# Attention stage of a hybrid block on one core: row scores, transposed scores and biases cut into 64x64 array tiles, the bias table split by head parity

## The chip, the core and the metric

The kernel runs on one core of one Trainium2 chip. The metric is the device time of one execution in microseconds (us), less is better. The core has TensorE (PE, with weight loads shown apart as PEld), VectorE (DVE), ScalarE (ACT), GpSimd (POOL) and the queue engine SyncE (SP), which issues most of the DMAs.

## What is computed

The block is attention, a mixture-of-experts layer, a Mamba layer and the same mixture-of-experts layer again. The change touches attention alone, for 2 sequences of 1024 tokens, 128 channels, 16 heads of 8 channels:

```python
def _L0_attn_a_ref(x, w_in, kernel_offsets, kernel_amplitudes, kernel_sharpness):
    ...
    q, k, v = (heads(q_), heads(k_), heads(v_))
    bias = tisa_bias(kernel_offsets, kernel_amplitudes, kernel_sharpness, l)
    scale = 1.0 / np.sqrt(HD).astype(np.float32)
    logits = jnp.einsum('bhld,bhmd->bhlm', q, k) * scale + bias[None]
    attn = jax.nn.softmax(logits, axis=-1)
    out = jnp.einsum('bhlm,bhmd->bhld', attn, v)
    return out.transpose(0, 2, 1, 3).reshape(b, l, d)
x = x + _L0_attn_a_ref(_layernorm(x, axis=-1), ...)
```

The bias of a head depends only on the distance of query and key (a Toeplitz matrix).

## The kernel before, in words

Every logit is computed twice. Once as **rows** (queries on the partitions, tile `at_rows`, three slots of a PSUM bank each), from which DVE takes each query's maximum with the bias table `table_max` (`pair_maxima`). Once as **columns** (keys on the partitions, tile `at_cols`, four banks): `scores` multiplies keys by queries, with the negated maximum in three further rows of the contraction (51 rows in all), and `biases` adds the bias by a matmul of `flip_sum` with the table `table_cols`. ACT takes the exponential into `prob`, and `products` multiplies `prob` by the values into `at_pv`.

Heads go in four groups of four; within a group two sequences; for each of them two halves of 512 queries and eight blocks of 128 keys. One (half, block) is a **step** (S = 0 to 127), and eight steps with one query half are a **phase** (16 phases). The q and k stacks hold the even heads of a group on partitions 0 to 47 and the odd ones on 64 to 111, so two matmuls (j = 0, 1) use the two halves of the array's rows.

The order on PE is written out by hand in `tensor_program`. A step is: one pair of row matmuls (`rows_pair`, n = 22 + 2S), the scores of both head pairs (hp = 0, 1), the biases of both, a second pair of rows, the products of the step before. In the third step of a phase the outputs of the phase before are turned (`turn_outputs`, L1308), in the seventh the negated maxima of the next one (`turn_maxima`, L1300). The last 11 steps have no rows left; there the order is scores, biases of hp 0, then scores, biases of hp 1. Waits: a row matmul waits until DVE has freed its slot (L1291); `scores(S, hp)` waits for the exponential of the step before and the same hp (L1316); ACT waits for the last bias matmul of hp (`cols_ready`).

`table_cols` holds for all four heads the high part of the bias on partitions 0 to 63 and the low part on 64 to 127; `flip_sum` (two reversed identities, one under the other) adds the two in one contraction over 128 rows. `load_table` (L1040) fills one of four chunks of columns by two DMAs from SP. Beside attention, weights of the next stage are split by POOL, and in the last two phases the first routing head of the next stage (`FfnHead`) runs among the steps.

Of the kernel before, what the change touches and what calls it, by code (L numbers as in the profile page):

```python
# [15 lines left out]
P = 128  # L16
# [879 lines left out]
def attention(m, x, w_in, offsets, amplitudes, sharpness, up_w, down_w, shared_up_w, shared_down_w,  # L896
# [3 lines left out]
    with ExitStack() as stage:  # L900
# [43 lines left out]
        t_col = sb("table_cols", [P, G4, COL_W], F16)  # L944
# [85 lines left out]
        def toeplitz(row, h0, nh, parts, c0, n):  # L1030

            a = row[h0:h0 + nh, c0:c0 + n]
            return bass.AP(tensor=a.tensor, offset=a.offset, ap=[[1, parts], [2 * L, nh], [1, n]])
# [6 lines left out]
        def load_table(eng, g, c):  # L1040
            for r, row in ((0, bias_hi), (HALF, bias_lo)):
                eng.dma_start(t_col[r:r + HALF, :, c * CW:(c + 1) * CW],
                              toeplitz(row, G4 * g, G4, HALF, c * CW, CW)).then_inc(tab_in[c], 16)
# [39 lines left out]
        with nc.Block() as block:  # L1083
# [147 lines left out]
            def tensor_program(pe):  # L1231
# [51 lines left out]
                def rows_pair(n):  # L1283

                    p, at = Pair(n), slots.start["pair", n]
                    if n % (2 * PHASE_PAIRS) == 0:
                        pe.wait_ge(stack_in[p.b], stack_count(p.g))
                    for j in range(2):
                        r = slice(HALF * j, HALF * j + QK_ROWS)
                        if at + j >= SLOTS:  # L1290
                            pe.wait_ge(slots_free, at + j + 1 - SLOTS)  # L1291
                        mm(s1[:, (at + j) % SLOTS, :], q_st[r, p.b, p.lh, p.hp, p.lbq * P:(p.lbq + 1) * P],  # L1292
                           k_st[r, p.b, p.hp, p.mh * BANK:(p.mh + 1) * BANK], start=True, stop=True).then_inc(fills, 1)
# [18 lines left out]
                def scores(S, hp):  # L1312
# [4 lines left out]
                    for j in range(2):  # L1317
                        r = slice(HALF * j, HALF * j + QK_ROWS + PIECES)
                        mm(s2[:, hp, j, :], k_st[r, b, hp, mb * P:(mb + 1) * P],  # L1319
                           q_st[r, b, lh, hp, :], start=True, stop=False)  # L1320

                def biases(S, hp):
                    for j in range(2):
                        for u in range(2):
                            c = step_columns(S % STEPS, u)
                            last = mm(s2[u * HALF:(u + 1) * HALF, hp, j, :], m.flip_sum[:],  # L1326
                                      t_col[:, 2 * hp + j, c:c + BANK], start=False, stop=True)
                    last.then_inc(cols_ready, 1)
# [29 lines left out]
                for S in range(ALL_STEPS):  # L1358
# [8 lines left out]
                    if pairs:  # L1367
                        for hp in range(2):
                            scores(S, hp)
                        if phase_turned_in(S) is not None:  # L1370
                            turn_maxima(phase_turned_in(S))
                        if it % BATCH == 0:
                            for c in range(CHUNKS):
                                if chunk_starts[c] == s:
                                    pe.wait_ge(tab_in[c], 32 * (it // BATCH + 1))
                        for hp in range(2):
                            biases(S, hp)
                        for n in pairs[1:]:
                            rows_pair(n)
                    else:  # L1380
                        for hp in range(2):
                            scores(S, hp)
                            biases(S, hp)
                            if hp == 0 and phase_turned_in(S) is not None:
                                turn_maxima(phase_turned_in(S))
# [700 lines left out]
```

## Time and profile before

| | |
|---|---|
| time, three runs | 1118.01, 1123.06, 1123.2 us (median 1123.06) |
| span of the profiled execution | 1119.0 us (the profile gives no other time of it) |
| TensorE busy in the span | 975.8 us, 87% |
| VectorE busy | 853.2 us, 76% |
| ScalarE busy | 677.5 us, 61% |
| GpSimd busy | 487.5 us, 44% |
| mean granted TensorE clock | 0.931 of full |

A busy share is an average over four stages. Attention lies between 0 and about 517 us; its 128 steps between 70 and 505 us. In a timeline a row is a run of the same instruction: start, length, engine, line, what is written and read, how often, and in brackets how long the engine idled before it and what ended that. Starts of matmuls are recorded, their ends are modelled, so distances between starts are what counts.

### The profile page before, as it was taken

Reading aid. Unit: us, or ns where it says so; the run is one execution under the profiler, and the core shown is the slowest. Engines: PE = TensorE matmul, PEld = TensorE weight load, DVE = VectorE, ACT = ScalarE, POOL = GpSimd, SP = SyncE. Lnnn points to the kernel's source line nnn. Section 1 sums busy time; section 2 is a strip of 40 time slices with the busy share of each in tenths; the row PEclk is TensorE's granted clock in tenths of the full one; section 3 lists DMA queues with packets and bytes.
Section 4 is the critical chain, followed back from the end, with each engine's and each line's share of the span. In section 5 each row is a group of like instructions: output and inputs, shape, how many; then the busy total and the mean of one; then the engine's idle time right before and its main releaser. Section 6 shows DMA issues by size and latency. Waiting matters only on the chain. (4 is left out here: it accounts for less than half of the span.)

```text
span 1119.0 us, 17095 instructions
## 1 busy us (share of the span) xinstructions
PE 975.8 (87%) x5565; PEld 543.6 (49%) x5565; DVE 853.2 (76%) x2203; ACT 677.5 (61%) x1042; POOL 487.5 (44%) x454
## 2 busy tenths in 40 slices
PE   4889999999999999994999999972777449999998
PEld 2413232223222322323777888731566337778886
DVE  7688888889888988766798555477897787975543
ACT  4226656565656565562668888768334126788886
POOL 4400101101110110101788999814674027889997
PEclk9559999999999999996999999987899659999999
DMA  4930224131313230003466677300000035676973
GB/s 100 281 107 9 79 71 85 35 101 55 71 34 104 53 70 2 1 2 87 143 177 175 160 198 191 96 20 1 0 0 0 3 93 151 172 179 158 218 197 96
DMA packets 80086, 105.65 MB, mean 94 GB/s; under 512 B 17741, under 2 KB 41091, under 8 KB 80003
## 3 DMA queue, kind: packets, MB, share of 16 engines
q1 hardware_dynamic: 78119, 102.42, 35.7%
q10 hardware_dynamic: 1883, 2.21, 0.7%
q8 instruction: 42, 0.69, 0.3%
q14 instruction: 42, 0.34, 0.1%
HBM read 95.84 MB, written 8.52 MB: 93 GB/s over the span
## 5 line engine op out<-in xcount | busy, mean ns | idle before, releaser
L663 POOL TENSOR_TENSOR f_act_low<-f_act,f_act_high 128x512 fp32r<-128x512 f32 x272 | 353.0, 1315 | 151.2 <-ACT f_act_high L639 143.5
L1506 DVE CUSTOM_DVE_ANT_0 at_rows<-at_rows,at_table_max 128x512 f32<-128x512 f32 x512 | 340.0, 718 | 43.6 <-PE at_rows L1292 42.9
L1452 ACT ACTIVATE at_prob<-at_cols 128x1024 f32<-128x1024 f32 x256 | 248.2, 1021 | 185.8 <-PE at_cols L1326 185.8
L678 DVE SCALAR_TENSOR_TENSOR f_gated<-f_hid,f_cw 128x512 f32<-128x512 f32 x256 | 174.0, 687 | 115.1 <-ACT f_act L644 86.9
L644 ACT ACTIVATE f_act<-f_gated 128x512 f32<-128x512 f32 x272 | 171.7, 631 | 110.2 <-DVE f_gated L678 78.5
L639 ACT CAST f_act_high<-f_act 128x512 fp32r<-128x512 f32 x272 | 164.7, 606 | 0.0
L1326 PE MATMUL at_cols<-at_table_cols,flip_sum 128*64 128x512 f16 x1024 | 139.3, 389 | 0.0
L1338 PE MATMUL at_pv<-at_prob,at_v_stack 128*32 128x512 f32 x1024 | 137.2, 608 | 0.2 <-ACT at_prob L1452 0.2
L1292 PE MATMUL at_rows<-at_k_stack,at_q_stack 48*128 48x512 bf16 x512 | 122.5, 408 | 12.8 <-DVE at_maxima L1506 10.1
L610 PE MATMUL f_acc<-f_act_high,wd_high 128*128 128x512 f32 x272 | 109.4, 402 | 9.0 <-POOL f_act_low L663 8.8
L1292 PEld LDWEIGHTS at_rows<-at_k_stack,at_q_stack 48*128 48x128 bf16 x512 | 28.9, 93 | 170.2 <-DVE at_maxima L1506 116.8
L610 PE MATMUL f_acc<-f_act_low,wd_high 128*128 128x512 f32 x272 | 106.8, 393 | 0.0
L610 PE MATMUL f_acc<-f_act_high,wd_low 128*128 128x512 f32 x272 | 106.7, 392 | 0.0
L600 PE MATMUL f_hid<-f_x_high,wu_high 128*128 128x512 f32 x204 | 81.9, 401 | 0.0
L1319 PE MATMUL at_cols<-at_q_stack,at_k_stack 51*128 51x512 bf16 x512 | 80.7, 382 | 0.7 <-ACT at_prob L1452 0.7
L1220 POOL CAST wu_high<-at_raw_weights 128x512 fp32r<-128x512 f32 (+1 forms) x9 | 5.3, 591 | 173.6 <-DMA at_raw_weights<-in_L_ffn_down_w_dram 154.0
L600 PE MATMUL f_hid<-f_x_high,wu_low 128*128 128x512 f32 x204 | 80.7, 395 | 0.0
L600 PE MATMUL f_hid<-f_x_low,wu_high 128*128 128x512 f32 x204 | 80.6, 395 | 0.0
L1326 PEld LDWEIGHTS at_cols<-at_table_cols,flip_sum 128*64 128x64 f16 x1024 | 48.1, 109 | 64.6 <-issue 42.1
L1506 DVE DVE_READ_ACCUMULATOR2_ANT at_maxima<- 128x1 f32 x512 | 71.8, 140 | 0.0
L1200 POOL COPY at_v_stack<-at_v_nat 128x256 f32<-128x256 f32 x8 | 3.1, 398 | 152.6 <-PE at_pv L1338 144.6
L610 PEld LDWEIGHTS f_acc<-f_act_high,wd_high 128*128 128x128 f32 x272 | 51.4, 189 | 28.5 <-POOL f_act_low L663 18.3
(322 smaller groups left out, 1351.0 us busy)
## 6 DMA issues: line engine op xcount, KB each, us to landing
f_cw<-f_c_rows SPq DMA_DIRECT2D x256, 256.0 KB, 4.5
at_table_cols<-bias_rows SPq DMA_DIRECT2D x32, 248.0 KB, 5.1
at_table_max<-bias_rows SPq DMA_DIRECT2D x12, 480.0 KB, 4.6
at_q_stack<-q_parts SPq DMA_DIRECT2D x32, 96.0 KB, 2.5
at_k_stack<-k_parts SPq DMA_DIRECT2D x24, 96.0 KB, 3.8
at_raw_weights<-in_L_ffn_up_w_dram SPq DMA_DIRECT2D x8, 256.0 KB, 4.3
at_raw_weights<-in_L_ffn_down_w_dram SPq DMA_DIRECT2D x8, 256.0 KB, 4.9
at_table_max<-bias_rows ACTq DMA_DIRECT2D x4, 480.0 KB, 8.0
```

Source lines behind the costliest of these rows:

```text
L600: last = nc.tensor.matmul(hid[:, n % HID_SLOTS, :], w[:, unit.pp, :], x[:, cols], start=(k == 0), stop=(k == 2))
L610: last = nc.tensor.matmul(acc[:, unit.j, :], w[:, unit.pp, :], x[:, s, :], start=(unit.pp == 0 and k == 0), stop=(unit.pp == NPAIRS - 1 an ...
L639: nc.scalar.copy(act_h[:, n % PART_SLOTS, :], act[:, n % ACT_SLOTS, :]).then_inc(u.high_done, 1)
L644: nc.scalar.activation(act[:, n % ACT_SLOTS, :], gated[:, n % GATE_SLOTS, :], ACT.Square).then_inc(u.square_done, 1)
L663: nc.gpsimd.tensor_tensor(act_l[:, n % PART_SLOTS, :], act[:, n % ACT_SLOTS, :], act_h[:, n % PART_SLOTS, :].bitcast(F32), ALU.subtract).t ...
L678: ins = nc.vector.scalar_tensor_tensor(out=gated[:, n % GATE_SLOTS, :], in0=hid[:, n % HID_SLOTS, :], scalar=0.0, in1=cw[:, k % C_SLOTS, u ...
L1292: mm(s1[:, (at + j) % SLOTS, :], q_st[r, p.b, p.lh, p.hp, p.lbq * P:(p.lbq + 1) * P], k_st[r, p.b, p.hp, p.mh * BANK:(p.mh + 1) * BANK], s ...
L1319: mm(s2[:, hp, j, :], k_st[r, b, hp, mb * P:(mb + 1) * P], q_st[r, b, lh, hp, :], start=True, stop=False)
L1326: last = mm(s2[u * HALF:(u + 1) * HALF, hp, j, :], m.flip_sum[:], t_col[:, 2 * hp + j, c:c + BANK], start=False, stop=True)
L1338: last = mm(pv[32 * h:32 * h + 32, :], vst[:, it % 2, LT - 1 - s % LT, h, :], prob[:, S % 2, h, :], start=(s % LT == 0), stop=(s % LT == L ...
L1452: act(prob[:, S % 2, 2 * hp:2 * hp + 2, :], s2[:, hp, :, :], ACT.Exp).then_inc(exp_done, 1)
L1506: nc.vector.tensor_tensor_reduce(out=slot, in0=slot, in1=t_max[:, 2 * p.hp + j, c:c + BANK][:, ::-1], scale=1.0, scalar=-3.0e38, op0=ALU.a ...
```

## The change

Three matmuls become 64x64 tiles. `rows_pair` and `scores` split their 128 output partitions into two matmuls of 64 (c, u), so a set of four matmuls covers the four quarters of the array. `table_cols` becomes [half by head parity][piece][head pair][column]: even heads on partitions 0 to 63, odd ones on 64 to 127, high and low part behind one another. `biases` takes 64 rows for each matmul and adds the high and the low part one after the other, 16 matmuls instead of 8. `load_table` issues four DMAs of half the size for each chunk. The order of the last 11 steps becomes that of the others (scores of both hp, then biases of both).

```diff
-        t_col = sb("table_cols", [P, G4, COL_W], F16)
+        t_col = sb("table_cols", [P, 2, G4 // 2, COL_W], F16)
...
         def load_table(eng, g, c):
-            for r, row in ((0, bias_hi), (HALF, bias_lo)):
-                eng.dma_start(t_col[r:r + HALF, :, c * CW:(c + 1) * CW],
-                              toeplitz(row, G4 * g, G4, HALF, c * CW, CW)).then_inc(tab_in[c], 16)
+            for j in range(2):
+                for piece, row in enumerate((bias_hi, bias_lo)):
+                    eng.dma_start(t_col[HALF * j:HALF * (j + 1), piece, :, c * CW:(c + 1) * CW],
+                                  toeplitz(row, G4 * g + j, G4 // 2, HALF, c * CW, CW)).then_inc(tab_in[c], 16)
...
-                        mm(s1[:, (at + j) % SLOTS, :], q_st[r, p.b, p.lh, p.hp, p.lbq * P:(p.lbq + 1) * P],
-                           k_st[r, p.b, p.hp, p.mh * BANK:(p.mh + 1) * BANK], start=True, stop=True).then_inc(fills, 1)
+                        for c in range(2):
+                            q0 = p.lbq * P + c * HALF
+                            last = mm(s1[c * HALF:(c + 1) * HALF, (at + j) % SLOTS, :],
+                                      q_st[r, p.b, p.lh, p.hp, q0:q0 + HALF],
+                                      k_st[r, p.b, p.hp, p.mh * BANK:(p.mh + 1) * BANK], start=True, stop=True)
+                        last.then_inc(fills, 1)
...
-                        mm(s2[:, hp, j, :], k_st[r, b, hp, mb * P:(mb + 1) * P],
-                           q_st[r, b, lh, hp, :], start=True, stop=False)
+                        for u in range(2):
+                            k0 = mb * P + u * HALF
+                            mm(s2[u * HALF:(u + 1) * HALF, hp, j, :], k_st[r, b, hp, k0:k0 + HALF],
+                               q_st[r, b, lh, hp, :], start=True, stop=False)
 
                 def biases(S, hp):
-                    for j in range(2):
-                        for u in range(2):
-                            c = step_columns(S % STEPS, u)
-                            last = mm(s2[u * HALF:(u + 1) * HALF, hp, j, :], m.flip_sum[:],
-                                      t_col[:, 2 * hp + j, c:c + BANK], start=False, stop=True)
+
+                    for piece in range(2):
+                        for j in range(2):
+                            half = slice(HALF * j, HALF * (j + 1))
+                            for u in range(2):
+                                c = step_columns(S % STEPS, u)
+                                last = mm(s2[u * HALF:(u + 1) * HALF, hp, j, :], m.flip_sum[half, :],
+                                          t_col[half, piece, hp, c:c + BANK], start=False, stop=piece == 1)
                     last.then_inc(cols_ready, 1)
...
-                    else:
-                        for hp in range(2):
-                            scores(S, hp)
-                            biases(S, hp)
-                            if hp == 0 and phase_turned_in(S) is not None:
-                                turn_maxima(phase_turned_in(S))
+                    for hp in range(2):
+                        biases(S, hp)
+                    for n in pairs[1:]:
+                        rows_pair(n)
```

On PE, one step in the middle of the kernel before reads as follows: rows, scores, biases, rows, products (the shape is output partitions x columns).

```order
L1292 MATMUL at_rows<-at_k_stack,at_q_stack 128x512 x2
L1319 MATMUL at_cols<-at_q_stack,at_k_stack 128x512 x4
L1326 MATMUL at_cols<-at_table_cols,flip_sum 64x512 x8
L1292 MATMUL at_rows<-at_k_stack,at_q_stack 128x512 x2
L1338 MATMUL at_pv<-at_prob,at_v_stack 32x512 x4
```

The same step of the changed kernel, in which the lines of the file have moved on:

```order
L1295 MATMUL at_rows<-at_k_stack,at_q_stack 64x512 x4
L1326 MATMUL at_cols<-at_q_stack,at_k_stack 64x512 x8
L1336 MATMUL at_cols<-at_table_cols,flip_sum 64x512 x16
L1295 MATMUL at_rows<-at_k_stack,at_q_stack 64x512 x4
L1348 MATMUL at_pv<-at_prob,at_v_stack 32x512 x4
```

The order of the five groups is the same; rows, scores and biases now have the same output width, and twice the matmuls.

On PE, one of the last 11 steps of the kernel before:

```order
L1319 MATMUL at_cols<-at_q_stack,at_k_stack 128x512 x2
L1326 MATMUL at_cols<-at_table_cols,flip_sum 64x512 x4
L1319 MATMUL at_cols<-at_q_stack,at_k_stack 128x512 x2
L1326 MATMUL at_cols<-at_table_cols,flip_sum 64x512 x4
L1338 MATMUL at_pv<-at_prob,at_v_stack 32x512 x4
```

And of the changed one:

```order
L1326 MATMUL at_cols<-at_q_stack,at_k_stack 64x512 x8
L1336 MATMUL at_cols<-at_table_cols,flip_sum 64x512 x16
L1348 MATMUL at_pv<-at_prob,at_v_stack 32x512 x4
```

Here the biases of hp 0 have moved behind the scores of hp 1.

On SP's queue, the first load of the table (the difference, - before, + changed), ahead of the stores of the second sequence's parts and the send of the first maxima:

```order
-L1115 DMA at_k_stack<-at_two_ones 3x16x128 x2
-L1042 DMA at_table_cols<-bias_rows 64x4x496 x8
+L1116 DMA at_k_stack<-at_two_ones 3x16x128 x2
+L1043 DMA at_table_cols<-bias_rows 64x2x496 x16
 L1025 DMA k_parts<-at_parts 128x3x1024
```

The number of table DMAs doubles and each has half the heads; nothing else in this queue changes place.

## Rows read from the trace of the kernel before

**Rows 1.** Page, part 1: busy us, share of the span, instructions.

```profile
PE 975.8 (87%) x5565; PEld 543.6 (49%) x5565; DVE 853.2 (76%) x2203; ACT 677.5 (61%) x1042; POOL 487.5 (44%) x454
```

**Rows 2.** Windows: length, busy us (instructions) of each engine, clock, DMA share, GB/s.

```profile
70.00:505.00 435.00, 423.66 (x3196) 128.00 (x3195) 372.46 (x1184) 260.49 (x277) 38.03 (x46) 0.99 0.20 50
...
180.34:206.74 26.40, 26.04 (x203) 7.93 (x201) 23.57 (x75) 15.99 (x17) 0.40 (x1) 1.00 0.28 60
...
148.46:151.52 3.06, 3.06 (x26) 0.83 (x25) 2.78 (x8) 1.81 (x3) 0.00 (x0) 1.00 0.02 4
...
866.06:871.06 5.00, 5.00 (x48) 5.00 (x47) 3.92 (x16) 2.23 (x4) 0.00 (x0) 1.00 0.01 3
```

**Rows 3.** Timeline of PE, one step, from scores to the next scores.

```profile
149.68 0.60 PE L1319 MATMUL at_cols<-at_q_stack,at_k_stack 51*128 51x512 bf16 x4
150.21 1.05 PE L1326 MATMUL at_cols<-at_table_cols,flip_sum 128*64 128x512 f16 x8
151.20 0.39 PE L1292 MATMUL at_rows<-at_k_stack,at_q_stack 48*128 48x512 bf16 x2
151.52 1.06 PE L1338 MATMUL at_pv<-at_prob,at_v_stack 128*32 128x512 f32 x8
152.51 0.39 PE L1292 MATMUL at_rows<-at_k_stack,at_q_stack 48*128 48x512 bf16 x2
152.74 0.60 PE L1319 MATMUL at_cols<-at_q_stack,at_k_stack 51*128 51x512 bf16 x4
```

**Rows 4.** Timeline, 150.44 to 150.46 us: a weight load while bias matmuls run.

```profile
150.45 0.11 PEld L1326 LDWEIGHTS at_cols<-at_table_cols,flip_sum 128*64 128x64 f16 x2
```

**Rows 5.** Timeline of ACT, and of PEld, in the next step.

```profile
151.79 1.02 ACT L1452 ACTIVATE at_prob<-at_cols 128x1024 f32<-128x1024 f32 x1
153.93 1.94 ACT L1452 ACTIVATE at_prob<-at_cols 128x1024 f32<-128x1024 f32 x2 [1.12 <-PE at_cols L1326]
...
152.86 0.10 PEld L1319 LDWEIGHTS at_cols<-at_q_stack,at_k_stack 51*128 51x128 bf16 x2 [0.24 <-ACT at_prob L1452]
```

**Rows 6.** Timeline of DVE, then PE, in the step after an output turn.

```profile
188.89 0.14 DVE L1506 DVE_READ_ACCUMULATOR2_ANT at_maxima<- 128x1 f32 x1
...
189.11 0.39 PE L1292 MATMUL at_rows<-at_k_stack,at_q_stack 48*128 48x512 bf16 x2
```

**Rows 7.** Timeline of DVE, then PE, behind the chain that negates the maxima.

```profile
196.91 0.69 DVE L1506 CUSTOM_DVE_ANT_0 at_rows<-at_rows,at_table_max 128x512 f32<-128x512 f32 x1
...
196.96 0.39 PE L1292 MATMUL at_rows<-at_k_stack,at_q_stack 48*128 48x512 bf16 x1
197.71 0.39 PE L1292 MATMUL at_rows<-at_k_stack,at_q_stack 48*128 48x512 bf16 x1 [0.36 <-DVE at_maxima L1506]
```

**Rows 8.** Timeline of PE: the turn of the maxima.

```profile
199.78 0.24 PE L1300 MATMUL at_rows<-identb,at_negm 128*48 128x128 bf16 x1
199.79 1.09 PE L1326 MATMUL at_cols<-at_table_cols,flip_sum 128*64 128x512 f16 x8
```

**Rows 9.** Timeline of PE in the last steps: products of two neighbouring steps.

```profile
489.94 1.07 PE L1338 MATMUL at_pv<-at_prob,at_v_stack 128*32 128x512 f32 x8
...
492.68 1.07 PE L1338 MATMUL at_pv<-at_prob,at_v_stack 128*32 128x512 f32 x8
```

**Rows 10.** Timeline of DVE: the first work behind the last products.

```profile
505.04 0.26 DVE L1542 RECIPROCAL at_rden<-at_rows 128x16 f32<-128x16 f32 x1 [8.80 <-PE at_rows L1308]
```

**Rows 11.** Timeline of SP's queue around the first table load.

```profile
41.59 5.41 SPq L1042 DMA_DIRECT2D at_table_cols<-bias_rows  x8
...
51.16 2.18 SPq L1025 DMA_DIRECT2D q_parts<-at_parts  x1
64.49 0.79 SPq L1058 DMA_DIRECT2D at_q_stack<-at_negT  x1
```

**Rows 12.** Timeline, 326 to 336 us: the longest stall of a step.

```profile
328.82 1.13 DVE L1524 CAST at_negm<-at_mtop 128x16 bf16<-128x16 f32 x1
...
331.43 0.53 PE L1292 MATMUL at_rows<-at_k_stack,at_q_stack 48*128 48x512 bf16 x1 [2.00 <-DVE at_maxima L1506]
```

More of the change, by code:

```diff
@@ L1030, in toeplitz @@
         def toeplitz(row, h0, nh, parts, c0, n):
-            a = row[h0:h0 + nh, c0:c0 + n]
-            return bass.AP(tensor=a.tensor, offset=a.offset, ap=[[1, parts], [2 * L, nh], [1, n]])
+            a = row[h0:h0 + 1, c0:c0 + n]
+            return bass.AP(tensor=a.tensor, offset=a.offset, ap=[[1, parts], [2 * 2 * L, nh], [1, n]])
         def load_max_tables(eng, g, hp):
@@ L1366, in tensor_program @@
                         pe.wait_ge(max_in[s // LT], 32 * (it + 1))
-                    if pairs:
-                        for hp in range(2):
-                            scores(S, hp)
-                        if phase_turned_in(S) is not None:
-                            turn_maxima(phase_turned_in(S))
[L1372 to L1376, printed above, removed]
-                            biases(S, hp)
-                        for n in pairs[1:]:
-                            rows_pair(n)
-                    else:
-                        for hp in range(2):
-                            scores(S, hp)
-                            biases(S, hp)
-                            if hp == 0 and phase_turned_in(S) is not None:
-                                turn_maxima(phase_turned_in(S))
+                    for hp in range(2):
+                        scores(S, hp)
+                    if phase_turned_in(S) is not None:
+                        turn_maxima(phase_turned_in(S))
+                    if it % BATCH == 0:
+                        for c in range(CHUNKS):
+                            if chunk_starts[c] == s:
+                                pe.wait_ge(tab_in[c], 64 * (it // BATCH + 1))
+                    for hp in range(2):
+                        biases(S, hp)
+                    for n in pairs[1:]:
+                        rows_pair(n)
                     if S > 0:
```

## The prediction

> **What bounds the kernel now.** First the busy shares: PE 87%, DVE 76%, ACT 61% of the whole span [rows 1]. That is a mean over four stages, so next the windows. In attention's 128 steps, 435 us, PE is busy for 423.7, DVE for 372.5, ACT for 260.5 [rows 2]. Within one undisturbed phase PE is busy 26.04 of 26.40 us and DVE 23.57, a reserve of 2.8 us for DVE; in one step PE is busy for all 3.06 us [rows 2]. The reader should see PE as the bound, but with DVE close behind.
>
> Next the timeline of one step [rows 3], read by distances between starts: scores to biases 0.53 us, biases to rows 0.99, rows to products 0.32, products to rows 0.99, rows to scores 0.23; sum 3.06. Between the last two groups the shape of the tiles does not change, and a set of matmuls that fill the array together costs 0.22 to 0.23; 512 columns at the upper clock of 2.4 GHz, which the granted clock of 1.00 in this step [rows 2] is, are 0.213. Scores are two such sets (0.43 to 0.44), biases four (0.85 to 0.88). So wherever the tile shape changes, 0.09 to 0.14 us are lost: scores to biases 0.09 to 0.10, biases to rows 0.11 to 0.14, rows to products 0.10, and a like amount inside the 0.99 of the products. That is what the change can remove.
>
> Last, who else is near. ACT: the weights of the second score group are loaded at 152.86, when the exponential that began at 151.79 and took 1.02 has ended (152.81); the biases start at 153.27, the next exponential at 153.93, and two of them take 1.94, to 155.87 [rows 3, 5]. From end to end that is 3.06 again: ACT's loop has hardly any more reserve than PE, though ACT is only 61% busy. (The start at 153.27 is one step of 3.06 behind the 150.21 of [rows 3].)
>
> **The change part by part.**
>
> *Work of the sets.* Rows stay one set for a pair (four quarter matmuls in place of two halves), scores two sets, biases four (16 quarters in place of 8 halves). If four quarters run together as two halves did, this costs nothing. PE has no such form in this trace; the nearest are the products, four tiles of 128x32 together, and the rows, two of 64x128. I take 0.
>
> *Changes of shape.* Of four in a step the two between scores, biases and rows go. With 0.22 for a set they are worth 0.09 + 0.11 = 0.20 us, with 0.213 they are 0.10 + 0.14 = 0.24 [rows 3]. I take 0.21, since a little comes back where 64-column weights must be loaded behind the products. PE's step is then 2.85.
>
> *Weight loads.* They double, four for each set. A load of 64 columns takes 0.11 us. The row at 150.45 stands in the middle of the bias matmuls, which run from 150.21 to 151.26: the load of a later matmul is hidden behind the one in flight, on the same rows of the array [rows 3, 4]. Taken as 0; if not hidden, the price is up to 0.11 a set.
> The Trainium skill (TensorE: Matmul & The Clock Gate, Part 3, What overlaps and what doesn't) states that weight loads overlap with matmuls in flight only if they go to another row group. By that rule each of the 8 sets would show its load, 0.9 us in a step. The trace speaks against it: the load at 150.45 overlaps on all 128 rows. I follow the trace.
>
> *ACT's loop.* The change takes the shape change out of it too: 152.86, one set 0.22, biases start, 0.64 to the exponential (0.66 now, less a little), 1.94, and 0.05 to the next load: 2.85. So ACT allows just the same step as PE.
>
> *DVE.* Two places in a phase don't follow PE. (a) Behind the output turn DVE works without a gap; the slot for the row matmul at 189.11 is free at 188.89 + 0.14 + some 0.05 = 189.08 [rows 6]. With a step shorter by 0.21 it would be wanted at 188.90: 0.18 of this step's 0.21 is given back. (b) Behind the chain that negates the maxima the second row matmul runs at 197.71, 0.80 after DVE took up its work at 196.91, instead of right behind the first at 196.96 [rows 7]. The start of DVE's chain hangs on an earlier row pair, so PE comes earlier and waits longer: this step's 0.21 is given back whole.
>
> *Turn of the maxima.* L1300 stands between scores and biases. Now it starts 0.01 ahead of the biases [rows 8], for both are narrow tiles over 128 rows; after the change it is a shape of its own between two equal ones, and a further change of 0.10 plus its own 128 columns, 0.05, comes in. This step keeps some 0.07.
>
> Phase of eight steps: five at 0.21, one at 0.03, one at 0, one at 0.07: 1.15 us. Thirteen undisturbed phases give 15.0. Of phase 0 six steps count, 1.2; of phase 14 the first three, 0.4, before the routing head's DVE work sets the pace. Sum 16.6.
>
> *The last 11 steps.* They take 2.74 now [rows 9], with six shape changes. PE would need less: 6 sets at 0.22, products 0.99 and 0.10 make 2.41. But the order is now both scores ahead of both biases, so the first exponential of a step hangs on the second one of the step before, and ACT's loop of 2.85 holds here too: 11 x 0.11 = 1.2 us lost. These steps do set the end: DVE sits idle for 8.80 us before it gets the last outputs [rows 10].
>
> *SP.* The first table load becomes 16 DMAs. Eight take 5.41 us to issue; 16 take between 5.4 (cost by size) and 10.8 (cost by piece), so up to 5.4 more. Behind them queue the stores of the second sequence, the last issued at 51.16 and done at 53.3, and the send of the first maxima at 64.49, which waits for DVE: 11 us of cover [rows 11]. Without that cover PE would start its steps late by the whole 5.4. Later loads come while a chunk is not wanted for four steps or more. 0.
>
> Sum: -16.6 + 1.2 = -15.4, say -15. The span was 1119.0 and the runs 1118.0 to 1123.2, median 1123.06, 4 us above the span, so the same difference from the median gives **1108 us**.
>
> **The rivals.**
>
> *DVE and ACT keep half.* If the two waits behind DVE grow and spread to their neighbours, or ACT's loop is 2.95 instead of 2.85 because the load at 152.86 must be finished before its matmul (0.10), the step is 2.95 and the gain 0.11: -8 + 2 (last steps), 1117 us. For it: two engines end within 0.05 us of each other in [rows 5]. Against: row matmuls at 197.71 start with their load, without 0.10 between. Chance 0.12.
>
> *No difference.* Quarter tiles cost a little each: 0.02 to 0.03 for each of 8 sets cancels 0.21. For it: with 64-column tiles the four sets of biases take 0.99, and I cannot say from groups how much of the 0.14 is the change of shape and how much the sets. 1117 to 1126, about 1122. Chance 0.16.
>
> *Slower, by weight loads.* The loads of four quarters don't hide: 8 x 0.11 = 0.87 in each of 117 steps, less the 0.21, and 6 x 0.11 in the last: +77 and +6, about 1205 us. It decides from 0.03 us a set. Against it [rows 4]. This is what the rule cited above would give. Chance 0.07.
>
> *Slower, by the feed of instructions.* A step would hold 32 quarter matmuls and 8 records of products, each with a load: 80 records in 2.85 us, 36 ns each. Now there are 51 in 3.06 (60 ns), and the densest 5 us of the whole trace have 95 (53 ns) [rows 2]; nothing in the trace shows 36 over a longer time. At 53 ns the step is 4.2 us: +1.2 x 117, about 1260 us. It decides above 38 ns. Against: weight loads of one set are recorded together, so PE itself takes them fast. Chance 0.08.
>
> *Slower by something small*, such as a lower granted clock for a while or the stall of [rows 12] at more places: there a cast of DVE took 1.13 us and PE waited 2.00. Where POOL's weight splits meet DVE's short chain depends on when each is due, and all moves. 3 us more or less in any case; 1130 to 1140 where it happens several times. Chance 0.05.
>
> **How the numbers follow.** The forecast has 0.49, half kept 0.12, no difference 0.16, the slower cases 0.20, and 0.03 is left for more than forecast: without (a) and (b), 117 x 0.21 = 24.6, 1100 us. A measurement of this kernel tells about 0.5%, 5.6 us, from no change. Faster holds the forecast, the larger gain and most of the half: 0.63. Same 0.17, slower 0.20. The forecast's own range is 1102 to 1114. The range for 8 in 10 begins at 1099 and reaches through "no difference" to 1127; the slower cases beyond (0.18) are left out.
>
> **What would show it.** Right: distances of starts in a plain step of 0.43 to 0.45 from scores to biases, 0.86 to 0.88 from biases to rows, unchanged 0.32 and 0.99; a step of 2.85, a phase of 25.2 to 25.3, DVE still busy for 23.6 of it; a row matmul waiting some 0.95 behind the negated maxima; 2.85 in the last steps, ACT idle between its pairs for 0.9. Wrong: biases to rows above 0.95 (sets or loads cost more), gaps in PE that nothing released (feed), a step at 3.06 with PE idle before the second scores (ACT) or before rows at all steps (DVE), the first step beginning later than now (SP).

## The result and the profile after

The changed kernel takes **1105.99 us** (median of four runs, 1103.68 to 1109.1) against 1121.36 us for the kernel before on the same chip (four runs, 1118.01 to 1123.2): a ratio of 0.989, 95% interval 0.986 to 0.9919. A second set of runs gave 1104.45 against 1118.28, 0.9871 [0.9837, 0.9905]. Forecast were 1108 us and 1099 to 1127.

The page, part 1, of the changed kernel (busy us, share of the span, instructions), whose profiled execution has a span of 1107.4 us and a time of 1109.1:

```profile
PE 957.4 (86%) x7613; PEld 561.8 (51%) x7613; DVE 855.9 (77%) x2203; ACT 677.8 (61%) x1042; POOL 487.8 (44%) x454
```

TensorE has 2048 matmuls more and is busy for 18 us less [rows 1]. Windows of one undisturbed phase and of one plain step (the columns of [rows 2]):

```profile
172.30:197.82 25.52, 24.98 (x333) 8.97 (x329) 23.65 (x75) 16.00 (x18) 2.07 (x3) 1.00 0.27 58
173.34:176.23 2.89, 2.89 (x45) 0.99 (x40) 2.75 (x9) 1.94 (x3) 0.79 (x2) 1.00 0.59 85
```

The phase fell from 26.41 (the 26.40 of [rows 2]) to 25.52, the step from 3.06 to 2.89; VectorE is busy for 23.65 us, nearly as before (23.57). Timeline of PE, the step that answers to [rows 3]:

```profile
173.34 0.64 PE L1326 MATMUL at_cols<-at_q_stack,at_k_stack 51*64 51x512 bf16 x8
173.81 1.04 PE L1336 MATMUL at_cols<-at_table_cols,flip_sum 64*64 64x512 f16 x16
174.67 0.39 PE L1295 MATMUL at_rows<-at_k_stack,at_q_stack 48*64 48x512 bf16 x4
174.99 1.07 PE L1348 MATMUL at_pv<-at_prob,at_v_stack 128*32 128x512 f32 x8
175.99 0.41 PE L1295 MATMUL at_rows<-at_k_stack,at_q_stack 48*64 48x512 bf16 x4
176.23 0.39 PE L1326 MATMUL at_cols<-at_q_stack,at_k_stack 51*64 51x512 bf16 x4
```

From scores to biases it is now 0.47 us (before 0.53), from biases to rows 0.86 (0.99), the other three 0.32, 1.00 and 0.24 (0.32, 0.99, 0.23). The 16 bias matmuls run as four sets of four and take 0.86, 0.215 a set; 512 columns at 2.4 GHz are 0.213. The ACT part of the same step, and the load of its second scores, which answer to [rows 5]:

```profile
172.50 1.02 ACT L1455 ACTIVATE at_prob<-at_cols 128x1024 f32<-128x1024 f32 x1
174.46 1.94 ACT L1455 ACTIVATE at_prob<-at_cols 128x1024 f32<-128x1024 f32 x2 [0.95 <-PE at_cols L1336]
...
173.57 0.11 PEld L1326 LDWEIGHTS at_cols<-at_q_stack,at_k_stack 51*64 51x64 bf16 x4 [0.32 <-ACT at_prob L1455]
```

The exponential ends at 173.52, the load of the second scores starts at 173.57, the biases 0.24 later at 173.81, the next exponential 0.65 after that, and two of them take 1.94. From end to end that is 2.89, the step. In steps in which the second scores don't wait, such as those whose scores start at 170.49 and 180.13 us, scores to biases is 0.43 instead of 0.47. So **ACT's loop sets the plain step now**, by a small margin over PE.

The last step's first exponential starts at 500.15 us before and at 485.81 after. Where these 14.3 us come from, by the distances of each step's first exponential:

| part | before | after | forecast of the difference |
|---|---|---|---|
| start of the steps | 73.00 | 70.60 | 0 |
| phase 0 | 27.61 | 26.44 | -1.2 |
| phases 1 to 13 | 347.85 | 336.51 | -15.0 |
| phase 14 | 31.47 | 31.52 | -0.4, and part of the +1.2 |
| phase 15 | 20.23 | 20.75 | part of the +1.2 |
| from there to the end | 618.8 | 621.6 | 0 |

The start and the end differ from run to run whatever the kernel: over all profiles here the start lies at 68.0 to 73.1, the rest at 617.0 to 621.8. What the edit did to the steps is the middle four rows: -11.9 us.

Two further profiles of the same work on PE, x8 below for the kernel before and the second one of the changed kernel, give -13.6 us for these rows.

An undisturbed phase, step by step:

| step | 1 | 2 | 3 | 4 | 5 | 6 | 7 | 8 | sum |
|---|---|---|---|---|---|---|---|---|---|
| before | 3.06 | 4.07 | 3.06 | 3.06 | 3.06 | 3.86 | 3.19 | 3.06 | 26.41 |
| after | 2.89 | 3.86 | 3.07 | 2.89 | 2.89 | 4.08 | 2.95 | 2.89 | 25.52 |

Step 2 (here by the order of its exponentials) holds the output turn, step 6 the chain that negates the maxima, step 7 their turn. PE in steps 6 and 7, which answers to [rows 7, 8]:

```profile
190.26 0.38 PE L1295 MATMUL at_rows<-at_k_stack,at_q_stack 48*64 48x512 bf16 x2
191.19 0.40 PE L1295 MATMUL at_rows<-at_k_stack,at_q_stack 48*64 48x512 bf16 x2 [0.54 <-DVE at_maxima L1509]
...
192.75 0.60 PE L1326 MATMUL at_cols<-at_q_stack,at_k_stack 51*64 51x512 bf16 x8
193.29 0.24 PE L1305 MATMUL at_rows<-identb,at_negm 128*48 128x128 bf16 x1
193.45 1.06 PE L1336 MATMUL at_cols<-at_table_cols,flip_sum 64*64 64x512 f16 x16
194.34 0.49 PE L1295 MATMUL at_rows<-at_k_stack,at_q_stack 48*64 48x512 bf16 x4
```

The second row matmul of the pair comes 0.93 behind the first (0.75 before), for PE arrives earlier and DVE does not. And DVE, the six operations of the chain:

```profile
189.06 0.14 DVE L1509 DVE_READ_ACCUMULATOR2_ANT at_maxima<- 128x1 f32 x1
189.24 0.18 DVE L1524 TENSOR_REDUCE at_mtop<-at_maxima 128x16 f32<-128x32 f32 x1
189.46 0.17 DVE L1525 TENSOR_SCALAR at_negm<-at_mtop 128x16 bf16<-128x16 f32 x1
189.67 0.17 DVE L1526 SCALAR_TENSOR_TENSOR at_mtop<-at_mtop,at_negm 128x16 f32<-128x16 f32 x1
189.88 0.17 DVE L1527 CAST at_negm<-at_mtop 128x16 bf16<-128x16 f32 x1
190.09 0.18 DVE L1528 TENSOR_TENSOR at_mtop<-at_mtop,at_negm 128x16 f32<-128x16 f32 x1
190.30 0.17 DVE L1529 CAST at_negm<-at_mtop 128x16 bf16<-128x16 f32 x1
190.38 0.69 DVE L1509 CUSTOM_DVE_ANT_0 at_rows<-at_rows,at_table_max 128x512 f32<-128x512 f32 x1
```

Each waits for the one before and so costs 0.21, though it works for 0.17. No row read starts between the accumulator read at 189.06 and 190.38; the slot that PE waits for is freed only behind it.

### The profile page after: what moved, and what is told of

It reads as the page before. It is cut to its first block and busy times, and to the rows that moved or that the text cites. A ratio compares the mean times of both kernels' runs of the same rounds, so it can differ in the third digit from the quotient of the medians.

```text
span 1107.4 us, 21223 instructions
## 1 busy us (share of the span) xinstructions
PE 957.4 (86%) x7613; PEld 561.8 (51%) x7613; DVE 855.9 (77%) x2203; ACT 677.8 (61%) x1042; POOL 487.8 (44%) x454
## 5 line engine op out<-in xcount | busy, mean ns | idle before, releaser
L1295 PE MATMUL at_rows<-at_k_stack,at_q_stack 48*64 48x512 bf16 x1024 | 128.3, 413 | 16.9 <-DVE at_maxima L1509 15.2
L1336 PE MATMUL at_cols<-at_table_cols,flip_sum 64*64 64x512 f16 x2048 | 135.4, 380 | 0.0
L1295 PEld LDWEIGHTS at_rows<-at_k_stack,at_q_stack 48*64 48x64 bf16 x1024 | 36.4, 107 | 146.1 <-DVE at_maxima L1509 124.7
L1326 PE MATMUL at_cols<-at_q_stack,at_k_stack 51*64 51x512 bf16 x1024 | 82.9, 387 | 2.9 <-ACT at_prob L1455 2.9
L1336 PEld LDWEIGHTS at_cols<-at_table_cols,flip_sum 64*64 64x64 f16 x2048 | 59.0, 107 | 42.3 <-issue 1.9
```

The costliest lines, as they stand in the source:

```text
L1295: last = mm(s1[c * HALF:(c + 1) * HALF, (at + j) % SLOTS, :], q_st[r, p.b, p.lh, p.hp, q0:q0 + HALF], k_st[r, p.b, p.hp, p.mh * BANK:(p.mh ...
L1326: mm(s2[u * HALF:(u + 1) * HALF, hp, j, :], k_st[r, b, hp, k0:k0 + HALF], q_st[r, b, lh, hp, :], start=True, stop=False)
```

## The experiments

The questions were four. Is the gain the removed changes of shape, and what is one worth (x1 to x4)? Does ACT's loop hold the step and the tail (x1, x5)? What holds steps 6 and 7 (x7, x9, x10)? What are the disturbed phases (x6)? In all of them "step" is the distance of first exponentials, from the trace. They ran in three sets, in which the kernel before had medians of 1116.82 us (x1 to x4), 1118.28 (x6 to x8 and the second runs of the changed kernel) and 1116.75 (x5, x9, x10); across sets the ratios are to be compared, not the times.

**x1: both orders on the changed kernel.**

```diff
-                    for hp in range(2):
-                        scores(S, hp)
-                    if phase_turned_in(S) is not None:
-                        turn_maxima(phase_turned_in(S))
...
                     for hp in range(2):
+                        scores(S, hp)
                         biases(S, hp)
+                        if hp == 0 and phase_turned_in(S) is not None:
+                            turn_maxima(phase_turned_in(S))
```

> The changed kernel with its 64x64 tiles, but in every step scores and biases of head pair 0, then scores and biases of head pair 1 (nothing is left out). Theory (ACT's loop holds the plain step at 2.89 us and the last steps too): the second scores now stand 0.43 us later, PE no longer waits for the exponential, a plain step falls to 2.85, a last step from 2.89 to about 2.41; about -4 and -5 us against the changed kernel's 1106, so 1096 to 1099. Rival (quarter tiles or the feed of instructions hold the step at 2.89): the steps stay at 2.89 and 1106 is measured.

1103.75 us (1100.55 to 1107.54), ratio 0.9875 [0.9846, 0.9903]. The plain step is 2.86, the last steps 2.42 instead of 2.89, but step 7 rose from 2.95 to 3.24, so the phase is 25.44. Expected were 1096 to 1099 us, and that did not come: phases 1 to 13 are only 0.4 us shorter than in the changed kernel (336.16 against 336.51), and the 3.8 us that phases 14 and 15 lose by the trace (48.52 against 52.27) do not stand out in the times. PE of one plain step of x1:

```profile
155.06 0.39 PE L1326 MATMUL at_cols<-at_q_stack,at_k_stack 51*64 51x512 bf16 x4
155.28 0.60 PE L1336 MATMUL at_cols<-at_table_cols,flip_sum 64*64 64x512 f16 x8
155.71 0.39 PE L1326 MATMUL at_cols<-at_q_stack,at_k_stack 51*64 51x512 bf16 x4
155.93 0.60 PE L1336 MATMUL at_cols<-at_table_cols,flip_sum 64*64 64x512 f16 x8
156.37 0.39 PE L1295 MATMUL at_rows<-at_k_stack,at_q_stack 48*64 48x512 bf16 x4
```

Between equal shapes a change of operand costs nothing: 0.22, 0.43, 0.22, 0.44. 2.86 is PE's own step, so ACT's loop costs the changed kernel 0.03 in a plain step and 0.47 in a last one.

**x2: the same order on the kernel before**, where it adds two changes of shape to each step.

```diff
-                        for hp in range(2):
-                            scores(S, hp)
-                        if phase_turned_in(S) is not None:
-                            turn_maxima(phase_turned_in(S))
...
                         for hp in range(2):
+                            scores(S, hp)
                             biases(S, hp)
+                            if hp == 0 and phase_turned_in(S) is not None:
+                                turn_maxima(phase_turned_in(S))
```

> The kernel before with only the order within a step changed: scores, biases of head pair 0, then scores, biases of head pair 1 (nothing left out). Two more changes of tile shape in each of 117 steps. Theory (each change costs about 0.1 us): step 3.26 instead of 3.06, 20 to 25 us slower than before, about 1143. Rival (the 0.09 to 0.14 belong to the bias matmuls themselves, such as their first weight load, and not to the change of shape): four sets of biases cost the same wherever they stand, under 5 us of difference.

1137.87 us (1135.17 to 1141.06), ratio 1.017 [1.0134, 1.0207]. The step went from 3.06 to 3.28, +0.22 for two more changes. PE of one step of x2:

```profile
152.77 0.38 PE L1319 MATMUL at_cols<-at_q_stack,at_k_stack 51*128 51x512 bf16 x2
153.08 0.62 PE L1326 MATMUL at_cols<-at_table_cols,flip_sum 128*64 128x512 f16 x4
153.64 0.39 PE L1319 MATMUL at_cols<-at_q_stack,at_k_stack 51*128 51x512 bf16 x2
153.96 0.62 PE L1326 MATMUL at_cols<-at_table_cols,flip_sum 128*64 128x512 f16 x4
154.51 0.39 PE L1292 MATMUL at_rows<-at_k_stack,at_q_stack 48*128 48x512 bf16 x2
```

Distances 0.31, 0.56, 0.32, 0.55, where x1 has 0.22, 0.43, 0.22, 0.44: each crossing costs 0.09 to 0.13, in both directions. In the 117 steps that have rows this order adds 21 us to the kernel before; x1 has it in these steps too (and in the last 11, where the kernel before had it all along) and stays about where the changed kernel was (0.9875, beside 0.989 and 0.9871): the change of shape is the price, not the order.

**x3 and x4: half of the change.** x3 is the changed kernel with the rows left 128 wide; its edit is shown. x4 has the rows and the scores left so, and only the biases and their table in 64x64.

```diff
-                        for c in range(2):
-                            q0 = p.lbq * P + c * HALF
-                            last = mm(s1[c * HALF:(c + 1) * HALF, (at + j) % SLOTS, :],
-                                      q_st[r, p.b, p.lh, p.hp, q0:q0 + HALF],
-                                      k_st[r, p.b, p.hp, p.mh * BANK:(p.mh + 1) * BANK], start=True, stop=True)
-                        last.then_inc(fills, 1)
+                        mm(s1[:, (at + j) % SLOTS, :], q_st[r, p.b, p.lh, p.hp, p.lbq * P:(p.lbq + 1) * P],
+                           k_st[r, p.b, p.hp, p.mh * BANK:(p.mh + 1) * BANK], start=True, stop=True).then_inc(fills, 1)
```

> The changed kernel with the row matmuls put back to two of 64x128, scores and biases left as 64x64. Theory (any difference of shape costs, width too): rows to scores and biases to rows get 0.1 us each back, step 3.05 to 3.08, about 1119 to 1122, all the gain gone. Rival (only the change between 128 and 64 rows of the array costs, the width is free): step stays at 2.89, 1106.

> The kernel before with the bias table split by head parity and 16 bias matmuls of 64x64, rows and scores left as 64x128, order of the last steps as changed. Theory (any difference of shape costs): as many changes as before, step 3.05, and the last steps a little slower: 1120 to 1124. Rival (only the number of rows matters): all three kinds have 64 rows, step 2.89, 1106.

x3: 1121.48 us, ratio 1.0033 [1.001, 1.0055], step 3.06. x4: 1122.5 us, ratio 1.0042 [1.0018, 1.0067], step 3.06. PE of one step of x3:

```profile
152.21 0.39 PE L1293 MATMUL at_rows<-at_k_stack,at_q_stack 48*128 48x512 bf16 x2
152.53 0.63 PE L1322 MATMUL at_cols<-at_q_stack,at_k_stack 51*64 51x512 bf16 x8
152.98 1.03 PE L1332 MATMUL at_cols<-at_table_cols,flip_sum 64*64 64x512 f16 x16
153.95 0.39 PE L1293 MATMUL at_rows<-at_k_stack,at_q_stack 48*128 48x512 bf16 x2
```

Rows to scores is 0.32 here, 0.24 in the changed kernel; biases to rows 0.97, there 0.86. Width alone, on equal array rows, is a change of shape. Parts of the edit give nothing: either way four crossings are left in a step. Only with all three alike do two go. Both halves are even a little slower than the kernel before. Part of it is the new order of the last steps, which they keep: phases 14 and 15 take 52.54 us in x3 and 53.56 in x4, 51.70 before.

**x8: the DMAs alone**, the kernel before with each table DMA cut in two.

```diff
-                eng.dma_start(t_col[r:r + HALF, :, c * CW:(c + 1) * CW],
-                              toeplitz(row, G4 * g, G4, HALF, c * CW, CW)).then_inc(tab_in[c], 16)
+                for h in (0, 2):
+                    eng.dma_start(t_col[r:r + HALF, h:h + 2, c * CW:(c + 1) * CW],
+                                  toeplitz(row, G4 * g + h, 2, HALF, c * CW, CW)).then_inc(tab_in[c], 16)
...
-                                    pe.wait_ge(tab_in[c], 32 * (it // BATCH + 1))
+                                    pe.wait_ge(tab_in[c], 64 * (it // BATCH + 1))
```

> The kernel before with each DMA of the bias table for the columns cut into two by head pairs, nothing else (nothing left out). Theory (hidden behind SP's idle time): 16 DMAs take 5 us more to issue at the start, the first exponential does not come later for it, no difference, within 3 us. Rival (SP's queue is on the path at the start or at a chunk change): 3 to 6 us slower, first exponential later or steps 5 or 13 of some group longer.

1119.63 us, ratio 1.0007 [0.9986, 1.0027]: no difference that can be told.

**x6: POOL's splits three steps later**, on x1.

```diff
-WEIGHT_STEPS = tuple(4 + 12 * k for k in range(1 + PAIRS // WPAIRS))
+WEIGHT_STEPS = tuple(7 + 12 * k for k in range(1 + PAIRS // WPAIRS))
```

> The changed kernel in the order of x1 (scores and biases head pair by head pair), and the steps in which SP loads the next stage's weights moved from 4 + 12k to 7 + 12k (nothing left out). Theory (the irregular steps, in x1 3.63, 4.30, 5.07, 4.18 and 4.76 us in phases 2, 8, 9, 11 and 12, come where POOL's weight split meets DVE's short dependent operations behind a phase's last maxima or its outputs): the splits fall elsewhere, these five go back to 3.07 and 3.83, phases 1 to 13 together 336.2 falls by about 4, time some 4 us under x1. Rival (they come of DMA traffic or of DVE itself): the same steps stay long.

1098.49 us (1096.29 to 1102.6), ratio 0.982 [0.9791, 0.9849], beside 0.9875 for x1; in the profiles phases 1 to 13 fell by 3.5 us (336.16 to 332.62), where 4 were expected. What the splits collide with shows in the changed kernel in phase 12, whose sixth step takes 5.14; DVE, PE and POOL there:

```profile
395.56 1.24 DVE L1525 TENSOR_SCALAR at_negm<-at_mtop 128x16 bf16<-128x16 f32 x1
...
398.35 0.40 PE L1295 MATMUL at_rows<-at_k_stack,at_q_stack 48*64 48x512 bf16 x2 [1.61 <-DVE at_maxima L1509]
...
395.50 1.27 POOL L1223 TENSOR_TENSOR wd_low<-at_raw_weights,wd_high 128x512 fp32r<-128x512 f32 x1
```

A DVE operation of 0.17 us took 1.24, from shortly after POOL's started to just after it ended, and PE's wait rose from 0.54 to 1.61. What phases 1 to 13 take above 13 times their median (0.9 us of it in phase 13, where the next stage's statistics start) is 4.5 us in the kernel before, 4.2 and 2.8 in two profiles of the changed one, 2.1 to 9.1 over the ten profiles with the splits in their old place, and 1.5, 1.8 and 1.6 in the three with the later splits (x6, x9, x10). It differs between runs of one kernel, so which step is hit, and how hard, is luck; that less is lost with the later splits holds in all three.

Not all of this is the wait itself. In the kernel before, PE waited 2.00 us in the stall of [rows 12], and behind it the granted clock was 0.51 from 331.50 to 335.00 us, that is 1.2 GHz nearly throughout. The products that start there take 1.93 us instead of 1.07:

```profile
331.89 1.93 PE L1338 MATMUL at_pv<-at_prob,at_v_stack 128*32 128x512 f32 x8
```

Of the 3.1 us by which this phase is too long, about half is the wait and half the lower clock. The same happened once in x8 and twice in x3, behind waits of 1.92 to 2.07 us, which is how x3 comes to 9.1. Behind the 1.61 us above, and behind 1.82 in x1, the clock stayed at 1.00; why it falls in one case and not in the other is not shown.

**x7: a short chain**, on the changed kernel. The expectation says what it leaves out.

```diff
-                    ch.link(ts(piece(0), top(0), -1.0, None, ALU.mult))
-                    ch.link(stt(out=top(1), in0=top(0), scalar=-1.0, in1=piece(0), op0=ALU.mult, op1=ALU.subtract))
-                    ch.link(nc.vector.tensor_copy(piece(1), top(1)))
-                    ch.link(tt(top(2), top(1), piece(1), ALU.subtract))
-                    nc.vector.tensor_copy(piece(2), top(2)).then_inc(negm_ready, 1)
+                    ch.add(ts(piece(0), top(0), -1.0, None, ALU.mult))
+                    ch.add(ts(piece(1), top(0), 0.0, None, ALU.mult))
+                    ts(piece(2), top(0), 0.0, None, ALU.mult).then_inc(negm_ready, 1)
```

> The changed kernel with the chain that negates the maxima cut from six dependent operations to four of which three do not wait for each other; the second and third part of the maxima are left as zero. Theory (the second row matmul behind the chain waits for DVE, so this step follows the chain's length): the chain is 0.4 to 0.5 us shorter, step 6 of a phase falls from 4.08 by just that to about 3.6, a phase to 25.1, 6 us in all. Rival (PE or ACT hold that step): 4.08 stays.

1093.93 us (1089.4 to 1095.92), ratio 0.9767 [0.9729, 0.9805]. From the first negation to the next row read it is 0.24 us now (184.50 to 184.74) instead of 0.92, and step 6 fell from 4.08 to 3.39, while all other steps stayed: the chain's length is this step's, one to one. The saving was underestimated: expected were 0.4 to 0.5 a phase and 6 us, measured 0.69 and, against the changed kernel in the same set (1104.45), 10.5. Nine of them are the step in 13 phases; phase 0 fell by more than its one step (from 26.88 to 23.74), because the clock rose earlier in it, as told at the end.

**x9: the same saving without leaving anything out**, on x6: the second part is written as bf16 straight from the sum.

```diff
-                    ch.link(stt(out=top(1), in0=top(0), scalar=-1.0, in1=piece(0), op0=ALU.mult, op1=ALU.subtract))
-                    ch.link(nc.vector.tensor_copy(piece(1), top(1)))
-                    ch.link(tt(top(2), top(1), piece(1), ALU.subtract))
-                    nc.vector.tensor_copy(piece(2), top(2)).then_inc(negm_ready, 1)
+                    ch.add(stt(out=top(1), in0=top(0), scalar=-1.0, in1=piece(0), op0=ALU.mult, op1=ALU.subtract))
+                    ch.link(stt(out=piece(1), in0=top(0), scalar=-1.0, in1=piece(0), op0=ALU.mult, op1=ALU.subtract))
+                    tt(piece(2), top(1), piece(1), ALU.subtract).then_inc(negm_ready, 1)
```

> On top of x6: in the chain that negates the maxima the first bf16 part and the rest below it are taken straight from the sum instead of one from the other, so 5 operations instead of 6 with one dependent step less. Theory (in each phase one step waits for the end of this chain, so its length is this step's): the sixth step of a phase falls from 3.83 to about 3.5, the phase from 25.4 to 25.1, 13 phases make 4 to 4.5 us: about 1094. Rival (DVE's next row reads are what the row pair waits for, not the chain itself): the step stays at 3.8 and the time at 1098.

**1092.01 us** (1086.53 to 1096.08), ratio 0.9773 [0.9747, 0.9799], the lowest median of a kernel that computes everything. Step 6 is 3.50, the phase 25.11. DVE in x9:

```profile
185.91 0.17 DVE L1524 TENSOR_SCALAR at_negm<-at_mtop 128x16 bf16<-128x16 f32 x1
186.12 0.18 DVE L1525 SCALAR_TENSOR_TENSOR at_mtop<-at_mtop,at_negm 128x16 f32<-128x16 f32 x1
186.21 0.17 DVE L1526 SCALAR_TENSOR_TENSOR at_negm<-at_mtop,at_negm 128x16 bf16<-128x16 f32 x1
186.41 0.17 DVE L1527 TENSOR_TENSOR at_negm<-at_mtop,at_negm 128x16 bf16<-128x16 f32 x1
186.51 0.69 DVE L1508 CUSTOM_DVE_ANT_0 at_rows<-at_rows,at_table_max 128x512 f32<-128x512 f32 x1
```

From the first negation to the first row read it is 0.60 here and 0.92 in the changed kernel (189.46 to 190.38): two operations that don't wait for each other start 0.09 apart, not 0.21. The 0.32 is the fall of step 6 (3.83 to 3.50). Between the profiles of x6 and x9, phases 1 to 13 are 4.4 us shorter, as expected, and phase 0 another 2.2, where the granted clock reached 1.00 some 4 us earlier (below). The medians are 6.5 us apart, the ratios of the two sets 5.

**x10: the turn beside the products**, on x9. The order of the slots and DVE's copy move with it (not shown).

```diff
+                    if phase_turned_in(S) is not None:
+                        turn_maxima(phase_turned_in(S))
                     for n in pairs[:1]:
                         rows_pair(n)
...
-                        if hp == 0 and phase_turned_in(S) is not None:
-                            turn_maxima(phase_turned_in(S))
```

> On top of x9: the turn of the maxima (128 columns, output of 48 partitions) moves from between scores and biases to the start of its step, directly behind the products, where the shape of the tiles changes in any case; the copy on DVE moves with it. Theory (each shape change costs 0.10 to 0.11 us wherever it stands): the seventh step falls from 3.24 to about 3.0 and 13 phases give 3 us: about 1091. Rival (the turn then waits for DVE's negated maxima, or the row pair behind it waits longer for its slot, since the turn takes a slot of the rows' bank): what is won is given back, 1094 or more.

1093.87 us (1088.52 to 1097.36), ratio 0.9787 [0.976, 0.9813]; x9 on the same chip 0.9773. Step 7 fell from 3.24 to 2.87, more than expected, but step 6 rose from 3.50 to 4.11, and the phase is 25.35 instead of 25.11: the rival, by the trace. The times alone can't tell the two apart, since their intervals overlap. PE and PEld in x10:

```profile
189.94 0.24 PE L1305 MATMUL at_rows<-identb,at_negm 128*48 128x128 bf16 x1
190.10 0.85 PE L1295 MATMUL at_rows<-at_k_stack,at_q_stack 48*64 48x512 bf16 x4
...
190.55 0.11 PEld L1295 LDWEIGHTS at_rows<-at_k_stack,at_q_stack 48*64 48x64 bf16 x2 [0.34 <-DVE at_maxima L1508]
```

The turn takes a slot of the rows' bank in a place where DVE is behind, so the second matmul of the pair behind it waits at 190.55 for a row read, and with it all of the step.

**x5: the tail alone**, the changed kernel with the old order in the last 11 steps.

```diff
-                    for hp in range(2):
-                        scores(S, hp)
...
-                    for hp in range(2):
-                        biases(S, hp)
+                    if pairs:
+                        for hp in range(2):
+                            scores(S, hp)
...
+                        for hp in range(2):
+                            biases(S, hp)
+                    else:
+                        for hp in range(2):
+                            scores(S, hp)
+                            biases(S, hp)
+                            if hp == 0 and phase_turned_in(S) is not None:
+                                turn_maxima(phase_turned_in(S))
```

> The changed kernel with only the order of the last 11 steps put back (scores and biases of hp 0, then of hp 1). Theory (ACT's loop of 2.89 sets these steps in the changed kernel, since both scores stand ahead of both biases): the last steps fall from 2.89 to the 2.42 that PE needs, 9 or 10 plain ones of them, 4 to 5 us less than the changed kernel, about 1100. Rival (in these steps the products, or the routing head's work on DVE, are what holds): the steps stay at 2.85 or more and the time at 1104 to 1106.

1101.9 us (1098.5 to 1104.1), ratio 0.9855 [0.9831, 0.988]. The last steps take 2.42, and phases 14 and 15 together 48.34 us instead of 52.27: 3.9 less, as the theory had it. This rests on the trace: the ratio is only 0.0016 below that of the changed kernel in another set (0.9871), less than the intervals are wide.

## Why the prediction was right

The 1108 us were 2 us from the median, and the mechanism was the one forecast. Its steps one by one:

*Sets and weight loads at 0.* Right. Four bias sets take 0.86 with four quarters each, and their 16 loads of 64 columns are hidden behind matmuls in flight:

```profile
173.65 0.71 PEld L1336 LDWEIGHTS at_cols<-at_table_cols,flip_sum 64*64 64x64 f16 x16
```

The weight-load rival fell, and with it the rule of the Trainium skill that was cited beside it (TensorE: Matmul & The Clock Gate, Part 3, What overlaps and what doesn't): here loads overlap matmuls on the same rows of the array.

*Two crossings worth 0.21.* Right: PE's own step is 2.86 (x1), 0.20 below 3.06; two more cost 0.22 (x2); four left give 3.06 (x3, x4). So in "no difference" the 0.02 to 0.03 a set is refuted too: the sets of 64 columns are not what the 0.99 held.

*ACT's loop 2.85.* The mechanism was right, the size off by 0.04: it is 2.89, the biases 0.24 behind the load and the exponential 0.65 behind them, where 0.22 and 0.64 were taken. In four of the eight steps this is what remains: 0.17 instead of 0.21. The half-kept rival's 2.95 did not come, since the second scores start with their load.

*DVE.* (a) Step 3 went from 3.06 to 3.07: all of its 0.21 was given back, 0.18 were forecast. (b) was half seen. The forecast was 0 for step 6 and -0.07 for step 7; measured +0.22 and -0.24. Only their sum is DVE's: 7.05 before, 7.03 after, 7.07 in x1, and between 7.03 and 7.16 in all ten profiles with the chain of six, where 6.98 was forecast. From 190.38 to 194.44 DVE has no gap, and the row pair at 194.34 takes 0.42 to the products instead of 0.32, since its second matmul needs the turn's slot, which DVE's copy frees then. So what the turn kept was given back there. Where the chain got shorter, the sum fell: 6.34 in x7, 6.74 in x9.

*Phase gain 1.15.* Mis-sized: 0.89. Four steps give 0.17, step 2 gives 0.21, steps 3, 6 and 7 nothing. This is the term of the sum that was off: -15.0 for 13 phases, of which the step sizes make -11.6 and the traces show -11.3.

*Phase 0 -1.2, phase 14 -0.4, last steps +1.2.* Measured -1.2, then +0.05 and +0.5 for phases 14 and 15. In the second pair of profiles phase 0 gives -1.1 (27.95 to 26.88); the two pairs can be compared, since in all four the clock rises 6 to 7 us behind the start of the phase. The last 10 distances sum to 31.03 before and 31.75 after, +0.7, for in the step with an output turn (3.76 to 3.43) the change also won something. x5 shows that the order costs 3.9 us there against the old one in the new shapes, which the forecast gave as PE's need of 2.41; 2.42 was measured. (The prediction counts six changes of shape in a last step of the kernel before; there are five, three among scores and biases and two at the products. Its sum does not use them.)

*SP 0.* Right, and the price by piece was the true one. SP's queue in the changed kernel, against [rows 11]:

```profile
42.96 10.47 SPq L1043 DMA_DIRECT2D at_table_cols<-bias_rows  x16
...
57.87 0.68 SPq L1025 DMA_DIRECT2D q_parts<-at_parts  x1
62.16 0.80 SPq L1059 DMA_DIRECT2D at_q_stack<-at_negT  x1
```

16 DMAs of half the size take 10.47 us to issue, 0.65 each; 8 took 5.41, 0.68 each. The last store ends at 58.55 and the send of the maxima at 62.16 still waits for DVE: of 11 us of cover some 4 are left.

*Instruction feed.* Fell: in the step shown above 40 matmul records and 40 loads pass in 2.89 us, 36 ns a record, with no gap in PE. (The 45 of the window count also matmuls of the neighbouring steps that reach into it, as do the 51 that the prediction takes from [rows 2]: that step has 48.) *Small clashes* stayed about as they were (4.5 us before, of which some 1.4 is the lower clock behind the stall; 4.2 and 2.8 after); x6 shows that most can be avoided.

So the steps gained 11.9 us, or 13.6 by the second pair of profiles, not 15.4. The medians differ by 15.4 and 13.8, with intervals from 9 to 18 us; the rest lies in what varies from run to run. That 1108 came within 2 us of 1106 is thus partly luck: with 11.9 us the same working would have given 1111, and its starting point, 1123.06, was itself 1.7 us above the median of the four runs.

## What to carry to other kernels

Read a tight PE loop by distances of starts, and look for what each place costs at which the tile's shape changes (here about 0.1 us); such a price is only saved by bringing all neighbours to one shape, not some. Before trusting the sum, write down the loops that run through other engines from end to end, with every hop: here ACT's was 0.03 above PE's new step, and DVE's chain fixed the sum of two steps. And when a change removes what an order was chosen to avoid, try the old order again: scores and biases by head pair cost 21 us in 117 steps in the old shapes; in the new ones they cost nothing there, and in the last steps they gain 4 by the trace.

## What the runs showed of the hardware that was not expected

- A change of width alone (64 to 128 output partitions or back, equal rows) costs 0.08 and 0.11 us in x3, and 0.10 and 0.13 in x4. Where mainly the array rows change, at the turn of the maxima, it is as much: 192.75 + 0.43 of scores end at 193.18 and the turn starts at 193.29; its 128 columns are 0.05 and the biases start 0.16 behind it. A change of operand, type and line within one shape costs nothing (x1).
- DVE operations of 16 columns that depend on each other start 0.21 apart, independent ones 0.09 (x9). One that meets a POOL operation can take 1.24 instead of 0.17.
- The granted clock in phase 0 reached 1.00 between 72 and 81 us in the profiles, and not by the work of PE just before it alone: x6 and x9 have PE busy for 5.85 us each from 66 to 72 us, with the same numbers of matmuls, yet x9 is at 1.00 (2.4 GHz) from 74 us and x6 from 78, both at 0.50 (1.2 GHz) until 72. Phase 0 took 26.44 us in x6 and 24.27 in x9. The windows of 2 us from 72 to 76 us, of x6 and then of x9:

```profile
72.00:74.00 2.00, 1.58 (x16) 0.38 (x12) 1.56 (x5) 1.17 (x2) 0.00 (x0) 0.50 0.01 4
74.00:76.00 2.00, 2.00 (x24) 0.93 (x18) 1.14 (x4) 0.79 (x1) 0.00 (x0) 0.50 0.03 8
```

```profile
72.00:74.00 2.00, 1.58 (x24) 0.47 (x20) 1.58 (x5) 1.15 (x2) 0.00 (x0) 0.79 0.00 0
74.00:76.00 2.00, 2.00 (x30) 0.52 (x22) 2.00 (x7) 1.67 (x2) 0.00 (x0) 1.00 0.04 12
```

What decides it stays open, and so these 2.2 us can't be ascribed to x9's edit.
